# Layer 1's spreads in a fused two-layer kernel: other pairs, and the gate and up products in other cycles

## The reference, cut to what matters

```python
x = x + attn0(layernorm(x)) + experts(layernorm(x))
xn = layernorm(x)
x = x + attn1(xn) + ffn(xn)

# attn0, for each channel c of 16 (rank 64):
qh = sigmoid(qz_u @ qz_v.T)                 # scores, 512 x 512
out += (qh @ qz_v) @ U + (qh.T @ qz_u) @ V

# attn1: q, k = elu(xn W) + 1, v = xn W; for every token t:
leaf = leaf + outer(k_t, v_t) in blocks of 4      # and Ws[l] + outer(UL k, VR v) on 4 levels
y_t = leaf q_t + sum of UL Ws VR q_t and UR Ws^T VL q_t on the 4 levels
out = y / max(sum(z * q), 1e-6) @ Wo

# ffn
h = silu(xn wg) * (xn wu); out = h @ wd           # hidden size 384
```

## Time and profile before

| | |
|---|---|
| median of 3 runs | 1568.86 us (1567.3 to 1570.67) |
| profiled execution | 1564.83 us, span 1563.0 us |
| granted TensorE clock, mean | 0.989 |
| PE busy | 1507.5 us, 96% of the span |
| DVE busy | 838.2 us, 54% |
| ACT busy | 753.3 us, 48% |

### The profile page before, as it was taken

One profiled execution on the slowest core, in us unless ns is written; L12 is line 12 of the kernel. 1 busy time (PEld: TensorE's weight loads), 2 busy tenths in 40 slices (PEclk: granted clock), 3 DMA queues, 4 the chain that ended last, 5 costly groups with the idle time before them and its releaser, 6 DMA issues.

```text
span 1563.0 us, 25542 instructions
## 1 busy us (share of the span) xinstructions
PE 1507.5 (96%) x8470; PEld 868.2 (56%) x8470; DVE 838.2 (54%) x1521; ACT 753.3 (48%) x1170; POOL 44.1 (3%) x41
## 2 busy tenths in 40 slices
PE   6999899999999999999999999999999999999977
PEld 3666554555555555655555555655555556555544
DVE  8868523445545555455445555455545554555446
ACT  3346455455444554454545544454535544455421
POOL 4000400000000000000000000000000000000000
PEclk9999999999999999999999999999999999999988
DMA  6002100000000000000000000000000000000000
GB/s 196 1 21 70 28 0 1 1 8 1 1 1 16 1 1 1 9 8 1 1 9 8 1 1 1 10 7 2 1 9 8 1 1 1 10 1 1 1 7 8
DMA packets 24096, 17.91 MB, mean 11 GB/s; under 512 B 1632, under 2 KB 22240, under 8 KB 23936
## 3 DMA queue, kind: packets, MB, share of 16 engines
q1 hardware_dynamic: 23600, 14.27, 3.2%
q0 software_dynamic: 336, 1.64, 0.3%
HBM read 11.70 MB, written 4.19 MB: 10 GB/s over the span
## 4 chain that ended last, share of the span: by engine, by line
issue 86%; PE 8%; DVE 4%; ACT 1%; POOL 1%; DMA 0%; DVEq 0%; SPq 0%; POOLq 0%; ACTq 0%
PE psum L1178 7%; DVE upper L644 0%; DVE upper L628 0%; DVE arena L869 0%; DVE upper L778 0%; DVE upper L776 0%; DVE upper L774 0%; DMA x_all<-in_x 0%; DVE upper L772 0%; ACT upper L1090 0%; DVE arena L875 0%; DVE upper L785 0%; DVE arena L787 0%; DVE arena L867 0%; DVE mv L648 0%
## 5 line engine op out<-in xcount | busy, mean ns | idle before, releaser
L1112 ACT ACTIVATE arena<-psum 128x1024 f32<-128x1024 f32 x504 | 476.1, 1030 | 617.7 <-PE psum L1178 617.7
L1178 PE MATMUL psum<-arena 128*64 128x512 f32 x2016 | 460.6, 599 | 0.3 <-DVE o_hl L820 0.3
L1178 PEld LDWEIGHTS psum<-arena 128*64 128x64 f32 x2016 | 133.4, 137 | 249.6 <-issue 238.6
L1178 PE MATMUL psum<-v_parts,u_parts 64*128 64x512 f32 (+1 forms) x1568 | 219.7, 407 | 0.0
L1178 PE MATMUL psum<-u_parts,v_parts 64*128 64x512 f32 x1536 | 212.2, 406 | 5.4 <-issue 4.6
L818 DVE TENSOR_SCALAR o_hl<-psum,sums 128x512 fp32r<-128x512 f32 x126 | 94.5, 750 | 225.9 <-PE psum L1178 225.9
L1178 PEld LDWEIGHTS psum<-v_parts,u_parts 64*128 64x128 f32 (+1 forms) x1568 | 144.5, 184 | 97.9 <-issue 51.1
L1178 PEld LDWEIGHTS psum<-u_parts,v_parts 64*128 64x128 f32 x1536 | 141.2, 184 | 99.7 <-issue 58.2
L875 DVE TENSOR_TENSOR arena<-psum,arena 128x512 f32<-128x512 f32 x96 | 65.6, 690 | 142.8 <-PE psum L1178 138.7
L976 ACT ACTIVATE arena<-psum 128x512 f32<-128x512 f32 (+3 forms) x186 | 103.9, 594 | 74.4 <-PE psum L1178 45.6
L820 DVE SCALAR_TENSOR_TENSOR o_hl<-psum,sums,o_hl 128x512 fp32r<-128x512 f32 x126 | 94.6, 751 | 4.5
(11 more groups left out here) (214 smaller groups left out, 1613.6 us busy)
## 6 DMA issues: line engine op xcount, KB each, us to landing
x_all<-in_x SPq DMA_DIRECT2D x4, 512.0 KB, 5.3
upper<-in_we SPq DMA_DIRECT2D x8, 256.0 KB, 2.7
expert_rows<-upper SPq DMA_DIRECT2D x16, 128.0 KB, 2.5
xn_s<-expert_rows SPq DMA_DIRECT2D x8, 256.0 KB, 2.8
out<-x_all SPq DMA_DIRECT2D x8, 256.0 KB, 2.7
arena<-in_e POOLq DMA_DIRECT2D x1, 896.0 KB, 5.1
arena<-in_wi POOLq DMA_DIRECT2D x1, 576.0 KB, 5.7
uT_w<-in_uT SPq DMA_DIRECT2D x1, 512.0 KB, 6.6
```

The costliest lines, as they stand in the source:

```text
L1112: nc.scalar.activation(th_of(un), psum[:, at:at + 2], ACT.Tanh, scale=0.5 * FACTOR_SCALE ** 2).then_inc(s_th, 2)
L1178: return nc.tensor.matmul(out, lhsT, rhs, start=start, stop=stop)
```

## The change

The spreads are grouped otherwise. Before, B of a level stood beside C of the level before, and D beside A of the next. Now C stands beside its own A, and D beside the next level's B. B0, B1, B2 and D6 stand alone. The first gate and up move from cycle 9 to 5, the second from 11 to 9; the third stays in 13. The y rounds of levels 3 and 4 come one cycle later (10 and 12), because their D does. One condition of the tail is written anew, so that a y round also stands ahead of the group of D6.

```diff
-ROWS_FIRST = {4: (("B", 0), ("A", 0)), 5: (("A", 1),), 6: (("A", 2),), 7: (("D", 2), ("A", 3))}
-ROWS_SECOND = {h: (("B", f + 1), ("C", f)) for h, f in ((4, 0), (5, 1), (6, 2), (7, 3), (9, 4), (11, 5))}
-ROWS_SECOND |= {h: (("D", f), ("A", f + 1)) for h, f in ((8, 3), (10, 4), (12, 5))}
-ROWS_SECOND[13] = (("C", NF - 1), ("D", NF - 1))
+ROWS = {4: [(("B", 0),), (("A", 0), ("C", 0))], 5: [(("B", 1),), (("A", 1), ("C", 1))], 6: [(("B", 2),)],
+        7: [(("A", 2), ("C", 2)), (("B", 3), ("D", 2))], 8: [(("A", 3), ("C", 3))], 9: [(("B", 4), ("D", 3))],
+        10: [(("A", 4), ("C", 4))], 11: [(("B", 5), ("D", 4)), (("A", 5), ("C", 5))], 12: [(("B", 6), ("D", 5))],
+        13: [(("A", 6), ("C", 6)), (("D", 6),)]}
-FULL_STEPS |= {h: [("gate", f), ("up", f)] for h, f in ((9, 0), (11, 1), (13, 2))}
+FULL_STEPS |= {h: [("gate", f), ("up", f)] for h, f in ((5, 0), (9, 1), (13, 2))}
...
             def row_spread(group, L, banks):
+                if ("B", 0) in group:
+                    wait_emptied(pe, ("v", 0), L)
                 if ("A", 0) in group:
-                    wait_emptied(pe, ("v", 0), L)
                     pe.wait_ge(s_stk, L + 1)
...
                     for group in TAIL_ORDER:
-                        kind, f = group[-1]
+                        kind, f = group[0]
                         if kind == "A" and f >= 3:
                             last_y_round(f - 3)
-                        if kind == "D" and f == NF - 1:
+                        if kind == "D":
                             last_y_round(ROUNDS - 2)
```

More of the change, by code:

```diff
@@ L65 @@
 HALVES = 2 * PAIRS
-ROWS_FIRST = {4: (("B", 0), ("A", 0)), 5: (("A", 1),), 6: (("A", 2),), 7: (("D", 2), ("A", 3))}
-ROWS_SECOND = {h: (("B", f + 1), ("C", f)) for h, f in ((4, 0), (5, 1), (6, 2), (7, 3), (9, 4), (11, 5))}
-ROWS_SECOND |= {h: (("D", f), ("A", f + 1)) for h, f in ((8, 3), (10, 4), (12, 5))}
-ROWS_SECOND[13] = (("C", NF - 1), ("D", NF - 1))
+ROWS = {4: [(("B", 0),), (("A", 0), ("C", 0))], 5: [(("B", 1),), (("A", 1), ("C", 1))], 6: [(("B", 2),)],
+        7: [(("A", 2), ("C", 2)), (("B", 3), ("D", 2))], 8: [(("A", 3), ("C", 3))], 9: [(("B", 4), ("D", 3))],
+        10: [(("A", 4), ("C", 4))], 11: [(("B", 5), ("D", 4)), (("A", 5), ("C", 5))], 12: [(("B", 6), ("D", 5))],
+        13: [(("A", 6), ("C", 6)), (("D", 6),)]}
 FULL_STEPS = {1: [("back", 0)], 2: [("norm", 0)], 3: [("kq", 0), ("v", 0)], 15: [("down", 0), ("den", 0), ("yo", 0)]}
-FULL_STEPS |= {h: [("gate", f), ("up", f)] for h, f in ((9, 0), (11, 1), (13, 2))}
+FULL_STEPS |= {h: [("gate", f), ("up", f)] for h, f in ((5, 0), (9, 1), (13, 2))}
 TAIL_ORDER = []
 for _h in range(HALVES):
-    TAIL_ORDER += [rows[_h] for rows in (ROWS_FIRST, ROWS_SECOND) if _h in rows]
+    TAIL_ORDER += ROWS.get(_h, [])
     TAIL_ORDER += [(s,) for s in FULL_STEPS.get(_h, [])]
@@ L130, in middle_of @@
         work = [w for w in work if w[0] != "norm"] + [("norm", 0)]
-    return [("rows", rows[h]) for rows in (ROWS_FIRST, ROWS_SECOND) if h in rows] + work
+    return [("rows", group) for group in ROWS.get(h, [])] + work
 def steps_of(work):
```

## The result

| | before | after |
|---|---|---|
| median | 1568.87 us (6 runs, 1565.00 to 1570.67) | 1559.23 us (6 runs, 1557.65 to 1561.47) |
| profiled execution | 1564.83 us, span 1563.0 | 1561.47 us, span 1559.7 |
| granted clock, mean | 0.989 | 0.991 |

The ratio is 0.9944 [0.9934, 0.9955]: 8.8 us less (the two medians are 9.6 apart), where 2.5 were forecast. The changed kernel was measured once more (experiment 3): 0.9956 [0.9943, 0.9969], 6.9 us. So the kernel is faster by 7 to 9 us, and the range of the prediction missed it.

The account below looks back on a forecast made before the run. The prediction took PE to bound the kernel, busy for 1507.5 of 1563.0 us. Seven loop turns (-1.75 us) and the tail (-0.75 us) gave -2.5 us, a median of 1566.4 us, range 1563.3 to 1569.8 us.

Parts of the forecast that it names:

- The loop, slot by slot: Loop cycles counted in passes of 512 columns: 44 slots before, 41 after; each turn -0.25 us.
- the slower rival: Cycle 5's chain on DVE comes late, once 0.35 us longer than worked out; +4.2 us, 1573.0 us, chance 0.07.
- net 0 of gate and up: In the loop, gate and up move from cycle 11 to 5 at the same price: net 0.
- Where cycle 4's gain goes: PE waits for add_g before cycle 5's scores, until +11.04; cycle 4 gains 0.28 us, not 0.61.
- 0.05 for the semaphore: Time added between add_g's end and cycle 5's scores for the semaphore: 0.05 us.
- 0.10 for weights that can't be loaded ahead: Time added before cycle 5's scores because the first weights can no longer be loaded ahead: 0.10 us.
- the loop's term: Seven turns of the loop at -0.25 us each: -1.75 us.
- the step that failed: In the tail, gate comes nearer behind y round 4: -0.75 us; the three fewer slots are mostly taken up by DVE.
- Both bounds of the tail: Limits set for the tail's gain: 0 and -1.6 us.
- The base: Profiled execution of 1564.83 us, 4.0 us under the median; forecast 1562.3 for it, median moved by the same amount.
- No wait in cycle 4: Rival: PE does not wait in cycle 4; a turn gives -0.58, with the tail -4.8, 1564.1 us; chance 0.20.
- Weights of lone passes are not hidden: Rival: lone passes take longer, so five fewer a turn save up to 8.4 us more; 1558.0 us, chance 0.03.

Follow-up runs that it names:

- experiment 3: Changed kernel measured once more, unaltered: ratio 0.9956 to before, 6.9 us less; also gates_only, ratio 0.9977.
- gates_only: Kernel before with old pairs, only gate and up moved to cycles 5, 9 and 13; ratio 0.9977 to before, -3.6 us.
- experiment 6: Kernels before and after, each with twelve extra products filling PE's waits in the tail; ratios to before 0.9991 and 0.9949.
- experiment 5: Changed kernel with the tail's y round 4 moved ahead of A6 and C6; ratio 0.9986 to before, tail 37.23 us.
- mixed kernel: Changed kernel's loop with the tail in the order of before; ratio 0.9980 to before, -3.1 us.
- y4_first: The kernel of experiment 5: changed kernel, y round 4 ahead of A6 and C6 in the tail; ratio 0.9986 to before.
- pairs_late_gates: Kernel before with the new pairs, gate and up in cycles 9, 10 and 13; ratio 0.9959 to before, tail 32.94 us.

## Why the prediction was wrong

**The loop, slot by slot: right.** The products with `uT_hl` start at +4.10 (forecast +4.14), cycle 5 is 10.17 long (10.19), cycle 6 11.31 (-0.65 against -0.67), cycle 11 9.57 (9.6). Cycle 5's chain is not late: DVE's line 896 ends at 708.67, and the next scores start at 709.38 without a wait. So the slower rival, with 0.35 us to spare, didn't come about. `gates_only` confirms the net 0 of gate and up in the loop.

**Where cycle 4's gain goes: right mechanism, size off.** PE does wait for `add_g`. The forecast was +11.04 for the next scores, and they start at +10.92. `add_g` ends at +10.86 (698.48 + 0.68 - 688.30), 0.03 ahead of what I had worked out. The 0.05 for the semaphore and the 0.10 for weights that can't be loaded ahead came from no row, and no run shows the 0.10: from the end of `add_g` to the first score are 0.06 us in all. With 0.07 in cycle 13 that makes -0.44 a turn instead of -0.25: the loop's term was 3.1 us and not 1.75.

**The tail: the step that failed.** It is the sentence "Three slots fewer, and at the low clock of the first stretch, are mostly taken up by DVE, whose work in the tail stays the same; the bounds are 0 and -1.6." DVE's work did stay the same (23.41 and 23.20 us). But DVE wasn't full: it waited 2.34 us for PE in that stretch, and the prediction reads PE's rows there and not DVE's. I saw y round 4 wait for DVE, took DVE for the later engine, and did not ask what DVE did next. It waited for C6, behind the same round. The experiments show in its place:

- the order alone gives 1.7 to 2.1 us, at nearly equal clock (experiment 6), and a y round 4 that stands ahead of A6 and C6 makes DVE wait again, 2.60 us (experiment 5);
- the rest goes with the clock. It returned 12 to 14 us behind the tail's first spread in all three traces of before and in the mixed kernel with the old tail, and 5 to 8 us behind it with the new pairs and unfilled waits. Two of the three traces of before, and the mixed kernel, have a second fall of 7 to 10 us around y round 4. With the new pairs only `y4_first` has one there (10.2 us), and none of those with C6 ahead of that round.

Both bounds of the tail were worked out at a fixed clock; the fall of the clock in the earlier trace rows was read as part of the scenery, though it depends on what PE does.

**The base.** I moved the median by the difference found against one trace. That execution was 4 us faster than the median, and this was no constant offset: it had the least idle time at the loop's branch (4.3 us against 7.1 and 7.0) and no second fall. The idle time is not touched by the change; the second fall is what the change removes, and that trace didn't show it.

**The rivals.** "No wait in cycle 4" (1564.1) was half right: the loop's gain was nearer to it, but the wait is there. "Weights of lone passes are not hidden" gave 1558.0, the number nearest to the result, by a mechanism that did not happen; its nearness is luck. The lone passes of B2 in the changed kernel start at 712.49, 712.72 and 712.95, 0.23 us apart at full clock, like those of A1 before, and the second one's weights (PEld) start to load as the first, on the same rows, starts:

```profile
712.49 0.18 PEld L1178 LDWEIGHTS psum<-val_low,e_high 64*128 64x128 f32 x1
```

Nothing in the loop was gained by fewer lone passes as such. The rule of the Trainium skill, "TensorE: Matmul & The Clock Gate", section "Part 3: Packing small matmuls", by which weights load under a running matmul only in another row group, disagrees with this trace as it did with that of before. The mechanism paragraph of the same section also lets weights for the background weight buffer pass ahead, and that fits the row above.

**Open.** Why the clock returns earlier with the new order is not settled. It returned at +9.0 in `gates_only`, at +7.3 in `pairs_late_gates`, and at +5.2 to +7.5 in the traces with both halves of the change, those with another bank or place of a y round among them. So the gates add nothing to the pairs that these traces could tell. Either may act through the length of PE's waits; no run separates this. With the second fall it is alike: every trace of the old pairs that has it shows y round 4 waiting for DVE ahead of it, but filling that wait brought no time. What PE's idle time at the loop's branch is, and why it differs between executions, stays open too.

## What to carry to other kernels

Where two engines take turns in waiting, read the waits of both before saying which one takes up a gain: an engine that is waited for can still have gaps of its own. Moving one product ahead of a wait can close them; the other engine's waits (1.49 and 1.21 us here) may stay and then cost nothing. Take a second and a third trace of the kernel before when a few microseconds matter, since one execution may lack the very stall that the change removes. And where the granted clock is below 1 next to the change, treat it as something that the change can move, with a bound of its own.

## What the hardware showed that I had not expected

- The granted clock fell a second time in the tail of two of three executions of the same kernel before, for 6.8 and 10.2 us, behind PE waits of 1.94 and 1.78 us for D5; the execution without it had waited 1.55. Gate then took 1.65 us instead of 0.97, and down 4.97 instead of 2.92 in the mixed kernel.
- Executions of one kernel differ in the loop too, at a clock of 1.00: 1167.7, 1170.2 and 1170.0 us for the same turns. The difference lies in cycles 15 and 0, around the loop's branch (12.4 to 13.0 and 10.4 to 11.0 us long), and is PE's idle time there, 4.3, 7.1 and 7.0 us in six branches, for which the profile shows no cause.
- A pass on the lower rows starts ahead of a pass on the upper rows that was issued before it: C0's first (691.51) starts ahead of B0's second (691.63). The rows don't name the half of the array; it follows from the 0.23 us between the other four starts (691.40, 691.63, 691.86, 692.08).
- Weights for the first score behind the wait for `add_g` cost nothing visible: 0.06 us from the end of DVE's row to the start of the product.
